# Taking weighted sums in pairs of key blocks, in a planned attention stage on one core

## The reference

```
scores = einsum('bhid,bhjd->bhij', q, k) / sqrt(16) - distance * slope[h], masked where j > i
attn   = softmax(scores, axis=-1)
out    = einsum('bhij,bhjd->bhid', attn, v) -> 2 x 2048 x 256, then @ o_w
x      = layernorm(x + out)
```

## Time and profile before

| | |
|---|---|
| time, median of 3 executions | 1443.52 us (1441.7 to 1443.78) |
| profiled execution | 1443.52 us, span of its instructions 1441.7 us |
| TensorE busy (matmuls) | 1387.3 us, 96% |
| VectorE busy | 1071.8 us, 74% |
| ScalarE busy | 869.8 us, 60% |
| GpSimd busy | 257.9 us, 18% |
| mean granted TensorE clock | 0.978 of full speed |

### The profile page before, as it was taken

How to read it: one execution, slowest core, us unless ns; L and a number is a source line. 1 busy time by engine, 2 the same in 40 slices (tenths; PEclk the granted TensorE clock), 3 DMA queues, 4 the chain that set the end, 5 groups by cost and what they waited for, 6 DMA issues and landing times. The chain is left out here.

```text
span 1441.7 us, 44126 instructions
## 1 busy us (share of the span) xinstructions
PE 1387.3 (96%) x18460; PEld 864.1 (60%) x18460; DVE 1071.8 (74%) x2004; ACT 869.8 (60%) x1775; POOL 257.9 (18%) x388
## 2 busy tenths in 40 slices
PE   7999999999999999999999999899987799999998
PEld 4554444444444444444444445788776689999997
DVE  2666888888888888888888880555788577767666
ACT  3445758788787787787777877655455233333342
POOL 4322111102110111021111110000356401111111
PEclk9999999999999999999999999999997599999999
DMA  7674511112212211122300000314424544454441
GB/s 220 201 176 137 91 33 38 44 30 51 46 32 47 44 36 45 31 50 46 92 3 3 3 3 2 116 43 164 165 84 143 195 180 161 174 183 181 175 181 73
DMA packets 77824, 134.08 MB, mean 93 GB/s; under 512 B 12226, under 2 KB 64443, under 8 KB 72252
## 3 DMA queue, kind: packets, MB, share of 16 engines
q1 hardware_dynamic: 59612, 108.84, 25.5%
q10 hardware_dynamic: 14608, 14.00, 3.0%
q0 software_dynamic: 3408, 8.43, 1.6%
HBM read 67.75 MB, written 23.11 MB: 63 GB/s over the span
## 5 line engine op out<-in xcount | busy, mean ns | idle before, releaser
L1798 DVE TENSOR_REDUCE part_max<-pair 128x2 f32<-128x1024 f32 (+2 forms) x576 | 643.7, 1161 | 82.2 <-PE pair L1216 44.7
L1610 ACT ACTIVATE big<-pair 128x512 f32<-128x512 f32 (+1 forms) x1120 | 585.1, 600 | 194.7 <-PE pair L1243 185.4
L1216 PE MATMUL pair<-big 128*32 128x512 bf16 (+3 forms) x5120 | 350.2, 348 | 2.4 <-DVE part_max L1798 2.2
L1243 PE MATMUL pair<-big 128*32 128x512 bf16 (+3 forms) x5120 | 342.1, 349 | 4.2 <-DMA big<-max_t 3.1
L1265 PE MATMUL pair<-big 128*17 128x512 f32 (+3 forms) x2560 | 288.2, 528 | 0.4 <-POOL big L2227 0.3
L1216 PEld LDWEIGHTS pair<-big 128*32 128x32 bf16 x5120 | 128.1, 96 | 179.8 <-DVE part_max L1798 83.0
L1243 PEld LDWEIGHTS pair<-big 128*32 128x32 bf16 x5120 | 126.4, 96 | 154.0 <-ACT big L1610 70.2
L1623 ACT ACTIVATE std<-moments,eps_col 128x1 f32<-128x1 f32 (+1 forms) x110 | 32.5, 295 | 218.7 <-DVE moments L1836 207.1
L1501 PE MATMUL pair<-big,tok 128*128 128x128 f32 x1248 | 148.3, 278 | 10.4 <-DVE big L2111 10.4
L1501 PEld LDWEIGHTS pair<-big,tok 128*128 128x128 f32 x1248 | 147.0, 194 | 13.8 <-DVE big L2111 12.1
L1513 PE MATMUL pair<-big 128*128 x624 | 141.0, 379 | 0.0
(11 more groups left out here) (184 smaller groups left out, 1310.6 us busy)
## 6 DMA issues: line engine op xcount, KB each, us to landing
tok<-big SPq DMA_DIRECT2D x39, 1024.0 KB
big<-in_L_ffn_w SPq DMA_DIRECT2D x16, 1024.0 KB
big<-split_dram SPq DMA_DIRECT2D x216, 64.0 KB, 2.8
split_dram<-big ACTq DMA_DIRECT2D x32, 384.0 KB, 4.1
big<-split_dram SPq DMA_DIRECT2D x42, 256.0 KB, 4.2
big<-routed_dram SPq DMA_DIRECT2D x39, 129.0 KB, 2.1
tok<-in_L_attn_x SPq DMA_DIRECT2D x8, 512.0 KB, 5.8
big<-in_c_query_rows SPq DMA_DIRECT2D x8, 512.0 KB, 4.7
```

The lines of the kernel that those rows point to most:

```text
L1216: mm = pe.matmul(bank[q:q + STRIPE, o:o + w], m.q_op[slot][:, step.qt, h, step.r * P + q:step.r * P + q + STRIPE], m.k_op[slot][:, h, step ...
L1243: mm = pe.matmul(m.bank[step.bank][k:k + STRIPE, n * w:(n + 1) * w], m.k_op[slot][:, h, step.kb * P + k:step.kb * P + k + STRIPE], m.q_op[ ...
L1610: act.activation(m.p_ring[:, step.place, step.heads[0]:step.heads[-1] + 1, step.at:step.at + w], m.bank[step.bank][:, 0:len(step.heads) * ...
L1798: dve.tensor_reduce(m.part_max[(step.u * QT + step.qt) % 2][:, step.r, step.heads[0]:step.heads[0] + n, step.c], banks[:, :, 0:w], X, ALU. ...
```

## The change

`weigh` takes a second block into the same step where one is there: it must be of the same query tile, its exponentials must be due by the planner's time, and its number must not be the first of four (the values of a block of four can come later than those of the four before). Nothing else is edited; the order that the planner writes out from there on follows from it.

```
     def weigh(self):
         blocks = [self.to_weigh.pop(0)]
+        while self.to_weigh and len(blocks) < 2 and self.to_weigh[0][1] == blocks[0][1] and self.to_weigh[0][-1] <= self.pe:
+            if self.to_weigh[0][2] % BPT == 0:
+                break
+            blocks.append(self.to_weigh.pop(0))
         u, qt = blocks[0][:2]
         first, last = blocks[0][2] == 0, blocks[-1][2] == (qt + 1) * BPT - 1
```

## The result

The changed kernel takes 1456.69 us (median of 6, 1447.69 to 1458.63) where the kernel before takes 1443.65 us in the same series: 1.0090 times, interval 1.0068 to 1.0112. It is slower by about 13 us, outside the range that was forecast.

A forecast was written before the change was run, and what follows sets the result against it. TensorE's work was taken to bound the front, with VectorE and ScalarE to be fed often enough. From 1443.52 us, minus 1.1 (borders) plus 0.5 (turns) gave 1442.9, rounded to 1443; range 1438 to 1450.

The forecast's parts named there:

- The borders: TensorE's switches from bf16 to fp32 and back around Weigh: each pair saves one, 1.1 us in all, at most 4.8.
- The price of a border: TensorE going from bf16 Score to fp32 Weigh and back: 0.00 to 0.03 us per border pair, 0.015 taken.
- A wait that comes earlier: A pair's first block also waits for the second's exponentials and selection: cost 0, bound 7 us.
- VectorE has enough slack for the pairs that are taken: From 200 to 861 us, 75 pairs use 65 of the 84.4 us VectorE has over: cost nothing.
- the price of dry pairs: Rival, engines run dry in double Weighs: 0.86 us per pair beyond 98, +53 us for all 160; chance 0.15.
- How many pairs: Of 320 Weigh steps, 177 meet the condition in the planner before; 50 to 90 pairs estimated, 75 taken.
- The gain of 1.1 us: Borders saved on TensorE: 75 pairs at 0.015 us each; outer bound 4.8 us, below 0.
- at the turn of a query tile: Where new exponentials wait for maxima by DMA, a shallower queue fills less: 0.5 us taken, bound 0 to 21 us.
- The rival with this mechanism: Pairs wait or the weigh queue is short at the turns: +5 us, 1448.5 us; chance 0.10.
- The first 200 us: From 45 to 200 us, TensorE idle 7.75 us; reordering bounded at 3 us either way, taken as 0.
- The end: The last blocks, waiting for GpSimd's selection and the copy of sums, are already weighed without a pause: 0.

The follow-up runs named there:

- the tenth experiment: The changed kernel with the planner made to wait until two blocks are ready, so all 320 blocks go in 160 pairs: 1499.04 us, 1.0385 times the kernel before.
- the eighth experiment: The changed kernel's order of instructions, but each block weighed in a step of its own: 1452.59 us, 1.0093 times the kernel before.
- the ninth: The kernel before, no pairs, no new block's scores begun while two blocks wait to be weighed: 1456.08 us, 1.0125 times the kernel before.
- the eleventh experiment: The kernel before with the planner keeping 1600 in place of 1200 ns of work ahead of VectorE: 1435.74 us, 0.9969 times the kernel before.
- The first three experiments: Third tile's maxima ahead of third unit's loads, changed kernel: 1.0065; loads ahead of maxima, kernel before: 1.0043; pairs in unit 0 alone: 1.0048.
- the first experiment: The changed kernel with the third query tile's maxima DMAs put ahead of the third unit's first operand loads: 1452.29 us, 1.0065 times the kernel before.
- the fifth experiment: Pairs allowed in units 6 and 7 alone (10 pairs): 1444.34 us, 1.0024 times the kernel before.
- the fourth: The changed kernel with no fold product allowed before the last maxima are sent (40 pairs in place of 38): 1451.78 us, 1.0059 times the kernel before.
- the second experiment: The kernel before, no pairs, with the third unit's first operand loads put ahead of the third query tile's maxima: 1449.62 us, 1.0043 times the kernel before.

## Why the prediction was wrong

**What held.** TensorE bounds the front: wherever it was made to wait, the time followed. The borders are cheap: no kernel got faster by having fewer of them, and the tenth experiment, with the fewest, is the slowest. The price of a border holds too: from 200 to 850 us of the kernel before, a group of L1243 is followed by Weigh after 0.225 us (median of 191) in place of 0.216, and the way back costs nothing (0.429 us, 153 times), so 38 borders are worth 0.4 us. *A wait that comes earlier* was put at 0, and the eighth experiment measures it: 1.0093 with single steps, 1.0090 and 1.0092 with pairs. That VectorE has enough slack for the pairs that are taken is right too (71.0 and 70.5 us of waiting), and the price of dry pairs was near: 53 us for all 160, measured 1.0385, some 56 us on 1444. That is in part luck, since the same reckoning gives nothing for 38 pairs, which cost 13 us.

**How many pairs.** 50 to 90 were estimated, 38 came. The reasoning, that each pair leaves the condition less often true, was right and its size too small. The gain of 1.1 us that hung on it is not seen.

**The step that failed: "at the turn of a query tile".** It says that "a queue that is shallower by one block has 0.86 us less to give", bounds this by 21 us, and takes 0.5 because "the view shows hardly a gap open now". That view shows how well the queue of the kernel before filled the gaps; it is no evidence about a kernel that has drained it. The queue stays at half its depth for the whole front, not for the one turn after a pair. (The 4.0 us of the view are also not all in weight loads: 1.0 us, 2 of the 6 times, are of the matmuls.) The loss was also not confined to turns: in the even stretch there are 48 more short waits than before, 8.2 us of them (6.1 net, against the 0.5 us taken), and the most frequent, 0.16 to 0.2 us each, fall at chunks whose room is still held. The rival with this mechanism got 0.10 and +5 us, at a quarter of its own bound. That the queue's depth is what makes the order dear is supported by the ninth and the eleventh experiment and by the count of ready blocks; both edits move other steps too, so it isn't shown as strictly as that the order is the cause.

**What could have been looked up.** The pairs were counted in the planner of the kernel before alone. The planner of the changed kernel can be run in the same way, and it says 38 pairs and last sums copied 7.0 us later than in the plan before (882.3 for 875.3 us of its own time); for all 160 pairs it says 52.8 us. Half of the loss was thus in the list's own arithmetic. The other half wasn't: it counts a fixed 3.0 us from a maximum to its landing (`ROWS_LAG`), whatever stands ahead on the DMA queue.

**"The first 200 us": bounded by 3 us either way, taken as 0.** The first three experiments put it at a loss of 4 to 7 us (0.25% less when mended, with overlapping intervals; 0.43 and 0.48% when made alone). The part had only looked at the waits for DVE at 185 us and not at SyncE's queue, though the planner's list orders DMAs as it orders matmuls. A Weigh step taken out of one place let 1 MB of loads pass 12 KB of maxima. Nor was the clock in it: in the changed kernel's profile the front has 10.2 us at half clock (6.8 behind this wait, 3.4 behind one at 60 us that comes ahead of any pair), in the profile before none. Where no wait fell on it (the first experiment) it had none either.

**"The end": 0.** It looked at the last weighed blocks and not at the filler. The profile of the fifth experiment puts the end at 5.1 us; by the fourth, the fold ahead of the send is some 2 of it. The changed order makes the way from the last maxima to the last sums 3.5 us longer in all (46.2 for 42.7 us); what the other 1.6 us of it and the rest of the 5.1 come from is open.

**The accounts.** Alone, the pairs of unit 0, of units 1 to 5 and of units 6 and 7 cost 0.48, 0.59 and 0.24%, in all 1.31%, and together 0.90%. The intervals are some 0.2 wide each way, so the difference of 0.41 is hardly outside the noise of four measurements; an overlap is possible, since a lead that is lost once can't be lost again, but it isn't shown.

## What to carry to other kernels

In a list order made by a planner, ask of an edit not what it saves where it stands but which reserve it uses up: the work that can be done at any time is the cover for every wait that can't be foreseen, and a view in which that cover works shows nothing of what is under it. Where the planner can be run, run it with the edit first: here its own count of time shows half of the loss. Ask also what passes what in every queue once one step is taken out, the DMA queue above all, where a small urgent transfer can end up behind a large one that nobody is waiting for. When an edit changes both an instruction and the order, build the order alone: one run said here that the pairs were innocent.

## What the runs showed of the hardware

Three DMAs of 4 KB landed in 1.8 us ahead of 1 MB of loads on the same queue and in 5.3 us behind them. An idle time of TensorE of 3.76 us was followed by 6.8 us at half clock in one profile (the changed kernel) and one of 3.69 us by 3.4 us in another (the second experiment), while 0.89 us had none behind it (the first). A wait of about 1 to 3 us at 60 us, ahead of the first weighed block and so ahead of any difference between the kernels, came out both ways in executions of the same order (1.30 us in the kernel before, 2.92 in the changed one) and moved the second maxima by 2 us: enough to hide or to feign an effect in a single profile.
